# Seeding the score banks three by ScalarE and one by VectorE, and summing every thirteenth probability tile on TensorE, in a fused cross-attention and feed-forward kernel

## The reference

```python
x0 = layernorm(x)                        # 2048 x 256
q, k, v = layer_norm(x0, g) @ Wq, ctx @ Wk, ctx @ Wv   # heads of 64; null key and value put in front
sim  = einsum('bhid,bhjd->bhij', q * s, k * s)         # 16 heads, 2048 x 1602
attn = softmax(sim)
out  = layer_norm(einsum('bhij,bhjd->bhid', attn, v) @ Wout, g_out)
x = x + out
h = concat([n, -n]) with n = layernorm(x)              # 512 -> 1024 -> 1024 -> 256, relu * 2 between
x = x + s2 * (relu(s1 * (relu(s0 * (h @ w0)) * 2 @ w1)) * 2 @ w2)
```

## Time and profile before

| | |
|---|---|
| median of 3 runs | 1356.48 us (1355.51 to 1357.03) |
| the profiled execution, its own time | 1355.39 us |
| its span | 1353.6 us |
| TensorE busy | 1308.8 us, 97% |
| VectorE busy | 916.3 us, 68% |
| ScalarE busy | 824.3 us, 61% |
| GpSimd busy | 956.1 us, 71% |
| the chain that ended last | TensorE 87%, VectorE 6%, ScalarE 3% of the span |
| mean granted clock of TensorE | 0.995 |

### The profile page before, as it was taken

The page is one execution under the profiler, slowest core; times in us unless marked ns, Lnnn a source line. Parts: engine busy times, 40 slices in busy tenths (PEclk is TensorE's granted clock), DMA queues, the critical chain, the costliest instruction groups (busy, mean ns, idle before and its releaser), DMA issues.

```text
span 1353.6 us, 19529 instructions
## 1 busy us (share of the span) xinstructions
PE 1308.8 (97%) x7292; PEld 683.6 (51%) x7292; DVE 916.3 (68%) x1078; ACT 824.3 (61%) x984; POOL 956.1 (71%) x480
## 2 busy tenths in 40 slices
PE   7989999999999999999999999999999879999998
PEld 3334444444444444444444444444444538787876
DVE  5457777777777777787778777877787555454432
ACT  3336767766767676677677666767789373324142
POOL 0008989999999999999999999999999471010100
PEclk9999999999999999999999999999999999999999
DMA  5241011110211121012012111201331220210000
GB/s 160 72 142 46 32 33 61 36 33 32 81 32 32 33 72 32 33 39 66 32 32 65 32 33 43 77 25 40 114 103 38 88 79 9 94 50 29 0 16 16
DMA packets 59731, 70.54 MB, mean 52 GB/s; under 512 B 14321, under 2 KB 42036, under 8 KB 59636
## 3 DMA queue, kind: packets, MB, share of 16 engines
q1 hardware_dynamic: 53780, 64.17, 15.1%
q10 hardware_dynamic: 5856, 5.11, 1.2%
HBM read 51.57 MB, written 17.69 MB: 51 GB/s over the span
## 4 chain that ended last, share of the span: by engine, by line
PE 87%; DVE 6%; ACT 3%; issue 2%; DMA 1%; SPq 0%; DVEq 0%; ACTq 0%
PE ps_o L1486 26%; PE ps_s L1473 19%; PE ps_x L1345 11%; PE ps_x L1580 7%; PE ps_s L1580 4%; PE ps_o L1403 4%; PE ps_s L1552 3%; DVE mxh L1073 3%; PE ps_s L1330 2%; PE ps_o L1392 2%; PE ps_o L1394 2%; PE ps_s L1332 2%; PE ps_x L1350 1%; PE ps_o L1425 1%; PE ps_x L1362 1%
## 5 line engine op out<-in xcount | busy, mean ns | idle before, releaser
L690 POOL TENSOR_TENSOR acc<-acc,prob 128x1024 f32<-128x1024 f32 x342 | 813.0, 2377 | 64.8 <-ACT prob L904 16.3
L1073 DVE TENSOR_REDUCE mxh<-ps_x 128x2 f32<-128x1024 f32 x374 | 457.5, 1223 | 200.3 <-PE ps_x L1345 194.2
L904 ACT ACTIVATE prob<-ps_s,keybias 128x1024 f32<-128x1024 f32 x416 | 441.0, 1111 | 186.9 <-PE ps_s L1473 186.7
L1486 PE MATMUL ps_o<-prob,vp 128*64 128x512 f32 x1664 | 405.2, 608 | 0.0
L1173 DVE COPY ps_s<-shift 128x1024 f32<-128x1024 f32 x208 | 253.5, 1219 | 35.2 <-ACT prob L904 24.0
L882 ACT ACTIVATE ps_s<-shift 128x1024 f32<-128x1024 f32 x208 | 213.7, 1028 | 0.6 <-DMA shift<-m_scratch 0.6
L1345 PE MATMUL ps_x<-kh,qh 64*128 64x512 f32 x748 | 185.1, 491 | 3.9 <-DVE mxh L1073 1.6
L1486 PEld LDWEIGHTS ps_o<-prob,vp 128*64 128x64 f32 x1664 | 101.4, 136 | 171.3 <-issue 158.4
L1473 PE MATMUL ps_s<-qh,kh 64*128 64x512 f32 x832 | 167.7, 398 | 8.9 <-ACT ps_s L882 6.1
L1345 PEld LDWEIGHTS ps_x<-kh,qh 64*128 64x128 f32 x748 | 69.7, 183 | 199.4 <-DVE mxh L1073 124.5
L1473 PE MATMUL ps_s<-ql,kh 64*128 64x512 f32 x832 | 164.8, 390 | 0.0
(11 more groups left out here) (160 smaller groups left out, 1185.6 us busy)
## 6 DMA issues: line engine op xcount, KB each, us to landing
shift<-m_scratch SPq DMA_DIRECT2D x32, 512.0 KB, 3.7
rb<-r_scratch SPq DMA_DIRECT2D x64, 128.0 KB, 2.9
o_scratch<-o_sb SPq DMA_DIRECT2D x32, 256.0 KB, 2.1
otb<-o_scratch SPq DMA_DIRECT2D x4, 2048.0 KB, 7.9
v_scratch<-vsb SPq DMA_DIRECT2D x13, 512.0 KB, 3.2
vp<-v_scratch SPq DMA_DIRECT2D x8, 832.0 KB, 5.4
xs<-in_x SPq DMA_DIRECT2D x4, 512.0 KB, 6.7
xres<-in_x ACTq DMA_DIRECT2D x1, 2048.0 KB, 8.9
```

The costliest lines, as they stand in the source:

```text
L690: gp.tensor_tensor(a, so_far, term, ALU.add).then_inc(sums_p, 1)
L904: act.activation(prob[:, slot(u, s), :, :], ps_s[s % S_BUFS][:, :, :], ACT.Exp, bias=keybias[:, kt:kt + 1], scale=SCALE).then_inc(p_made, 1)
L1073: dve.reduce_max(mxh[:, :, i // MXF, i % MXF], ps[:, :, 0:MXW], AX.X).then_inc(x_free, 1)
L1486: last = pe.matmul(ps_o[qb % 2][rows(g), :], vp[u][:, kt, rows(g)], prob[:, slot(u, s), g, :], start=(kt == 0), stop=(kt == KT - 1))
```

## The change

Seeding is shared out by bank instead of by step. In each cycle VectorE seeds head 0 of the even step (one bank, 512 columns), ScalarE head 1 of the even step and both heads of the odd step (three banks, in two instructions). `scores` waits for both engines' counters. From cycle 18 of the last pair on (`ALL_BY_VECTOR`) VectorE seeds all four banks in two instructions and ScalarE none.

The thirteenth tile (`kt` 12) of blocks 0 to 30 is no longer added by GpSimd: `sums` sums it on TensorE as a second term beside `acc`. The slot of that tile is then freed by L instead of by GpSimd. Block 30 loses its `add_four`; GpSimd adds its tiles 2 to 5 instead.

In the last pair the eight instructions that make `w1` on ScalarE move from cycles 6 to 13 to cycles 17, 18, 21 and 22, and the four that make `w0` on VectorE from cycle 18 to cycles 18, 19, 21 and 22.

```diff
-BY_VECTOR = {QB * PAIRS - 2: (2, 3, 4, 5), QB * PAIRS - 1: (5, 6, 7, 8)}
-BY_TENSOR = {QB * PAIRS - 1: (11, 12)}
+BY_VECTOR = {QB * PAIRS - 1: (5, 6, 7, 8)}
+BY_TENSOR = {b: (12,) for b in range(QB * PAIRS - 1)} | {QB * PAIRS - 1: (11, 12)}
+W1_AT = {17: (0, 1, 2), 18: (3, 4, 5), 21: (6,), 22: (7,)}
+W0_AT = {18: 0, 19: 1, 21: 2, 22: 3}
+ALL_BY_VECTOR = CYCLES * (PAIRS - 1) + 18
...
-def steps_of_bank(r, b):
-
-    return (KT * b + 1 - r) // 2
+def seeds_until(step):
+
+    k, odd = divmod(step, 2)
+    if k < ALL_BY_VECTOR:
+        return k + 1, 2 * k + 1 + odd
+    return ALL_BY_VECTOR + 2 * (k - ALL_BY_VECTOR) + 1 + odd, 2 * ALL_BY_VECTOR
...
@@ ScalarE
+            def seed(n, c):
+
+                if CYCLES * n + c >= ALL_BY_VECTOR:
+                    return
+                for s in (2 * c, 2 * c + 1):
+                    qb, kt = s // KT, s % KT
+                    if kt < 2:
+                        act.wait_ge(shift_set[qb], 16 * (n + 1))
+                    if n or c:
+                        act.wait_ge(p_made, STEPS * n + s + 1)
+                    elif s == 0:
+                        act.wait_ge(x_free, HEAD_X)
+                    else:
+                        act.wait_ge(vh_free, 2 * KT)
+                    heads = slice(0, 2) if s % 2 else slice(1, 2)
+                    act.activation(ps_s[s % S_BUFS][:, heads, :], shift[qb % 2][:, heads, :], ACT.Copy).then_inc(seeded_a, 1)
...
-                    if last and 6 <= c < 6 + FK:
+                    for k in W1_AT.get(c, ()) if last else ():
                         act.wait_ge(ld_raw, 48)
-                        act.activation(w1[c - 6][:, :], k1raw[:, c - 6, :], ACT.Identity, bias=minus_one[:, :], scale=2.0).then_inc(w1_made, 1)
+                        act.activation(w1[k][:, :], k1raw[:, k, :], ACT.Identity, bias=minus_one[:, :], scale=2.0).then_inc(w1_made, 1)
...
@@ VectorE
+            def seed(n, c):
+
+                alone = CYCLES * n + c >= ALL_BY_VECTOR
+                for s in (2 * c, 2 * c + 1) if alone else (2 * c,):
+                    qb, kt = s // KT, s % KT
+                    if kt < 2:
+                        dve.wait_ge(shift_set[qb], 16 * (n + 1))
+                    if n or c:
+                        dve.wait_ge(p_made, STEPS * n + s + 1)
+                    else:
+                        dve.wait_ge(x_free, HEAD_X)
+                    heads = slice(0, 2) if alone else slice(0, 1)
+                    dve.tensor_copy(ps_s[s % S_BUFS][:, heads, :], shift[qb % 2][:, heads, :]).then_inc(seeded_v, 1)
...
-                    if last and c == C_AT[0]:
-                        add_four(n, u, 2)
...
-                    if last and c == 18:
-                        split_small_weights()
+                    if last and c in W0_AT:
+                        split_small_weights(W0_AT[c])
...
@@ TensorE
-                pe.wait_ge(seeded[s % S_BUFS], CYCLES * n + s // 2 + 1)
+                by_vector, by_scalar = seeds_until(STEPS * n + s)
+                pe.wait_ge(seeded_v, by_vector)
+                pe.wait_ge(seeded_a, by_scalar)
```

More of the change, by code:

```diff
@@ L154, in sums_of @@
 def sums_of(b):
-    order = [kt for kt in range(KT) if kt not in BY_VECTOR.get(b, ()) + BY_TENSOR.get(b, ())]
-    return order + ["D"] if b in BY_VECTOR and b < QB * PAIRS - 1 else order
+    return [kt for kt in range(KT) if kt not in BY_VECTOR.get(b, ()) + BY_TENSOR.get(b, ())]
 def sums_until(b):
@@ L379, in xattn_ffn_kernel @@
         shift_stored, shift_set = sem("shift_stored"), [sem(f"shift_set{qb}") for qb in range(QB)]
-        seeded = [sem(f"seeded{r}") for r in range(S_BUFS)]
+        seeded_v, seeded_a = sem("seeded_v"), sem("seeded_a")
         mx_made, row_made = sem("mx_made"), sem("row_made")
@@ L521, in spread_shift @@
                 if b >= 2:
-                    for r in range(S_BUFS):
-                        sp.wait_ge(seeded[r], steps_of_bank(r, b - 1))
+                    by_vector, by_scalar = seeds_until(KT * (b - 1) - 1)
+                    sp.wait_ge(seeded_v, by_vector)
+                    sp.wait_ge(seeded_a, by_scalar)
                 sp.dma_start(shift[qb % 2][:, :, :], m_dram[n, qb].unsqueeze(0).broadcast_to([P, 2, QW])).then_inc(shift_set[qb], 16)
@@ L681, in add @@
                 kt = sums_of(b)[i]
[L682 to L687, removed]
+                gp.wait_ge(p_made, S_BUFS + STEPS * n + KT * qb + kt + 1)
+                term = prob[:, slot(u, KT * qb + kt), :, :]
                 gp.wait_ge(sums_p, sums_until(b) + i - 1)
@@ L897, in body @@
                             b = blocks(m, old // KT)
-                            if old % KT in BY_VECTOR.get(b, ()):
-                                act.wait_ge(sums_d, 2 * list(BY_VECTOR).index(b) + 2)
-                            elif old % KT in BY_TENSOR.get(b, ()):
+                            if old % KT in BY_TENSOR.get(b, ()):
                                 act.wait_ge(y_job_made, y_count(sums_job(plan, m - n, old // KT), pair) + 1)
@@ L906, in body @@
                     if c < CYCLES - 1:
-                        seed(n, 2 * c + 2)
+                        seed(n, c + 1)
                     elif not last:
@@ L1103, in add_four @@
                 dve.wait_ge(p_made, S_BUFS + STEPS * n + KT * qb + tiles[-1] + 1)
-                if b == QB * PAIRS - 1:
-                    dve.wait_ge(sums_p, sums_until(b))
                 for g in range(2):
@@ L1152, in attn_block_0, with split_small_weights @@
                 got.then_inc(y0_var, 1)
[L1154 to L1173, removed]
+            def split_small_weights(q):
+                if q == 0:
+                    dve.wait_ge(ld_raw, 48)
+                    dve.wait_ge(ld_g, 48)
+                    dve.wait_ge(pv_done, RING + STEPS * (PAIRS - 1))
+                    dve.tensor_scalar(s2x8[:, :], scol[:, 2:3], 8.0, None, ALU.mult).then_inc(s2_made, 1)
+                cols = slice(q * DIM, (q + 1) * DIM)
+                dve.tensor_tensor(w0[:, :, cols], k0raw[:, 0:DC, cols], k0raw[:, DC:2 * DC, cols], ALU.subtract).then_inc(w0_made, 1)
+            def seed(n, c):
[10 more added lines that the diff above has]
+                    dve.tensor_copy(ps_s[s % S_BUFS][:, heads, :], shift[qb % 2][:, heads, :]).then_inc(seeded_v, 1)
             def body(pair, plan, first, last):
@@ L1177, in body @@
                 if first:
-                    seed(0, 1)
+                    seed(0, 0)
                 for c in range(CYCLES):
@@ L1189, in body @@
                     if c < CYCLES - 1:
-                        seed(n, 2 * c + 3)
+                        seed(n, c + 1)
                     elif not last:
-                        seed(n + 1, 1)
-                    if last and c == C_AT[0]:
-                        add_four(n, u, 2)
+                        seed(n + 1, 0)
                     for j, i in plan[c]["C"]:
@@ L1275, in tail @@
                 if start:
-                    dve.wait_ge(sums_d, 4)
+                    dve.wait_ge(sums_d, 2)
                 for j in range(2, 8):
@@ L1493, in last_sums @@
                 pe.wait_ge(sums_p, sums_until(b + 1))
-                pe.wait_ge(sums_d, 4)
+                pe.wait_ge(sums_d, 2)
                 terms = [acc[(QB - 1) % 2], acc_d] + [prob[:, slot(u, STEPS - KT + kt), :, :] for kt in BY_TENSOR[b]]
```

## The result

| | before | after |
|---|---|---|
| median, us | 1355.99 (1355.31 to 1357.03) | 1363.31 (1362.32 to 1364.50) |
| ratio of the times | | 1.0057, 95% interval 1.0041 to 1.0073 |
| span of the profiled execution | 1353.6 | 1362.1 |

The kernel became slower by 7.3 us in the medians and by 8.5 between the two profiled executions, against a forecast of 1362.1 (+5.6). I read the difference cycle by cycle: for each of the 208 cycles, the start of its first score matmul in the one trace and in the other. The last cycle starts 8.4 later.

A forecast was written before the change was run, and what follows sets the result against it. The prediction took TensorE plus one reduction of the maxima to bound the kernel. Its terms, +13.3 - 0.9 - 5.6 - 1.5 + 0.5 - 0.2 = +5.6, gave 1362.1 us from 1356.5, range 1356.5 to 1368.5.

The forecast's parts named there:

- a term of 0.43: Thirteenth tile in 31 jobs L on TensorE: 0.43 us more each, +13.3 in all, upper end 17.7.
- Plain cycles: Cycles in the pairs: stay at 4.18 us, set by TensorE and one reduction, post waiting up to 0.2.
- Late seeds: Rival: first scores in 80 cycles start 0.3 late behind VectorE's one-bank copy, +8, hence 1370; chance 0.13.
- (a): Last pair: wait for otb gone and projection behind it at full speed, -5.6 (0 if the load waits otherwise).
- (b): Last pair, cycles without maxima: shorter TensorE waits for ScalarE's seed, -1.5 (0 to -4.2).
- (d): Last pair: w1 leaves cycles 6 to 13, where it stood before some exponentials, -0.2 (0 to -1).
- (c): Last pair, cycle 22: both VectorE seeds now stand behind attn_block_0, +0.5 (-0.5 to +2.5).
- VectorE's relief: Seeds in seven pairs: VectorE's shorter seed behind the rest of a query projection gives -0.9 (0 to -3.7).

The follow-up runs named there:

- doubled term: Changed kernel with tile 12 summed twice in every job L: 1377.03 us, span 1375.2 (one execution).
- two-block version: Changed kernel with the thirteenth tile on TensorE only in blocks 28 and 29 (31 as ever), others back on GpSimd: 1350.76 us, ratio 0.9957 to before.
- tile alone: Kernel before with only the thirteenth tile of blocks 0 to 30 moved to TensorE, seeds, w0 and w1 as before: 1366.76 us, ratio 1.0073.
- short reductions: Each reduction of the maxima over 256 of 512 keys: 1322.98 us in the changed kernel, 1350.71 in the kernel before (one execution each).
- exchanged banks: Changed kernel with VectorE seeding both banks of the even step and ScalarE both of the odd: 1382.72 us (one execution).
- seeds alone: Changed kernel with the sums as before, so only seeds and places of w0 and w1 changed: 1355.85 us, ratio 0.9992 to before.
- three-block version: Changed kernel, thirteenth tile on TensorE only in blocks 28 to 30 (31 as ever), some cycles' seeds reassigned, add_four split: 1341.55 us, ratio 0.9891 to before.

## Why the prediction was right, and where it was off

**The sign and the size.** Right: a term of 0.43 on the bound engine 31 times, and only one place, otb, where GpSimd's relief is worth something. The doubled term (+13.1), the two-block version (-12.6 against after) and the tile alone settle both halves.

**Plain cycles.** Right: they kept 4.18 to 4.20, since post waits for the reduction of pre and not for VectorE's seed. The short reductions show it from the other side. Of the step's own sizes the waiting was too small: I read up to 0.2 per cycle ahead of post, and none behind it; halving the reduction gave up to 0.27, of which 0.1 lay between post and the values.

**Late seeds.** The copy of one bank took 0.68 to 0.69, as taken from the row of 0.69, and the scores came no later. The exchanged banks show what it would have cost had it been 1.23.

**(a), (b), (d).** Right within 0.3: -5.4, -1.3, 0.0. The load of otb came 8.2 earlier against TensorE, a little more than the 4.8 to 7.1 forecast.

**(c) was mis-sized:** +0.5 forecast, +1.6 measured. I priced `attn_block_0` at its length before. But its first two operations took 4.48 instead of 3.64: GpSimd was adding block 31 beside the whole of them, and the add of 2.18 became one of 3.27. Idle for longer, TensorE also lost more to the lower clock (0.86 over 1085 to 1110 us, 0.93 before), where I had forecast a gain of 0.3. GpSimd's relief is one way into this, as the tile alone shows; the seeds alone show that the moved seeds and `w0` are another, and no run parts the two within the 4.48. The prediction never asked what a GpSimd that runs ahead would collide with.

**L in cycle 22 was missed:** 7 * 0.19 = +1.3. I followed every wait of the seeds, but not what is queued behind the longer seeds on ScalarE: `rowbuf`, for which L waits.

**VectorE's relief was larger:** -1.9 instead of -0.9, about 0.1 in each of cycles 13 and 21 and, in pair 5, 0.3 in cycles 12 and 13 together; inside its bounds (0 to -3.7). It makes up for most of the missed 0.19. That the forecast of +5.6 lies within 1.7 of the measured +7.3 is in part luck: three of its parts were off by 1.0 to 1.4 each, and not all the same way.

**Open:** why the clock falls more often at the start of the pairs in one execution than in another. Over 90 to 115 us it was 1.00 in the seeds alone and in the three-block version, 0.93 before, 0.86 after and 0.80 in the two-block version; no experiment changed only that.

## What to carry to other kernels

Give the bound engine work only at the places where the relieved engine is waited for: here two of 31 terms brought the gain, a third paid only once cycle 24 waited for GpSimd, and the others cost 0.43 each. When two limits lie 0.2 us a cycle apart, a change that moves the second alone measures as nothing or as its own cost, though it is worth much once the first is moved; shorten the first in a trial kernel before judging. And where a relieved engine runs ahead, look up what it will now run beside, and what is queued behind every instruction that is made longer.

## What the runs showed of the hardware

VectorE's addition of two 128x1024 float32 operands in SBUF took 1.38 with GpSimd nearly idle (one add of 0.32 beside it) and 3.27 beside GpSimd's adds, three of which took 9.01 instead of 3 * 2.38. A split for `w0`, also with two operands in SBUF, took 0.68 alone and 1.81 beside GpSimd's multiplication of `o_sb` and an add. ScalarE's copy of 512 elements took 0.60 and its seed of 1024 took 1.03, but two seeds behind each other, of 512 and 1024, took 1.55 and not 1.63.
